# Graph attention with edge attributes on one core: gathers up to three groups ahead, one product for messages and attributes, and the merge of an item moved into the next step

## What is computed

```python
xl = (x @ Wl + bl).reshape(n, heads, outc)
e_feat = jax.nn.leaky_relu(xl[src] + (x @ Wr + br).reshape(n, heads, outc)[dst], NEG_SLOPE)
logits = jnp.einsum('ehc,hc->eh', e_feat, att)
m = jax.ops.segment_max(logits, dst, num_segments=n)
a = jnp.exp(logits - m[dst])
denom = jax.ops.segment_sum(a, dst, num_segments=n)
a = a / denom[dst]
out = jax.ops.segment_sum(xl[src] * a[:, :, None], dst, num_segments=n)
```

## Time and profile before

| | us |
|---|---|
| median of 3 runs | 8522.77 |
| lowest, highest | 8516.57, 8523.01 |
| profiled execution | 8491.84 |
| its span | 8489.9 |

### The profile page before, as it was taken

The page is one execution under the profiler, slowest core; times in us unless marked ns, Lnnn a source line. Parts: engine busy times, 40 slices in busy tenths (PEclk is TensorE's granted clock), DMA queues, the critical chain, the costliest instruction groups (busy, mean ns, idle before and its releaser), DMA issues.

```text
span 8489.9 us, 109176 instructions
## 1 busy us (share of the span) xinstructions
PE 4879.8 (57%) x24176; PEld 4286.7 (50%) x24176; DVE 5222.4 (62%) x16308; ACT 4307.0 (51%) x10681; POOL 4740.8 (56%) x4843
## 2 busy tenths in 40 slices
PE   4666666666666655555555555545555555544446
PEld 3565656565656544444444444444444444444444
DVE  5555565656565656766666667655555555555556
ACT  3444444444454545555555555545555555555546
POOL 3555555555555545666666666656666666666640
PEclk7666666666666666766767767666666666666666
DMA  5333333333333322322322323222222222222221
GB/s 147 94 100 91 96 97 97 97 96 97 96 98 95 98 67 74 79 76 76 77 75 77 82 77 78 76 66 72 77 71 71 72 72 72 76 73 72 72 61 50
DMA packets 460163, 697.83 MB, mean 82 GB/s; under 512 B 140781, under 2 KB 330019, under 8 KB 460101
## 3 DMA queue, kind: packets, MB, share of 16 engines
q0 software_dynamic: 154752, 327.15, 16.9%
q1 hardware_dynamic: 305349, 370.00, 14.2%
HBM read 638.95 MB, written 57.76 MB: 82 GB/s over the span
## 4 chain that ended last, share of the span: by engine, by line
PE 33%; issue 27%; DVE 22%; another core or an unknown queue 7%; ACT 6%; POOL 3%; DMA 2%; SPq 0%; DVEq 0%; ACTq 0%; POOLq 0%
PE PS L791 14%; PE PS L763 10%; PE PS L783 6%; DVE z L1186 3%; POOL xl_g L706 3%; DVE am L1193 3%; DVE msg L1285 2%; ACT distT L931 2%; ACT ST L936 2%; DVE relu_logit L1202 1%; ACT dist L906 1%; PE PS L749 1%; DMA xl_g<-xl_tab,edges 1%; DVE relu_logit L1205 1%
## 5 line engine op out<-in xcount | busy, mean ns | idle before, releaser
L706 POOL DMA_INDIRECT xl_g<-xl_tab,edges x4836 | 4740.0, 980 | 3485.8 <-DVE z L1186 1689.1
L763 PE MATMUL PS<-xr_w,ST 128*128 128x132 f32 x9672 | 2054.2, 373 | 2160.7 <-issue 1278.8
L763 PEld LDWEIGHTS PS<-xr_w,ST 128*128 128x128 f32 x9672 | 1778.9, 269 | 2455.4 <-issue 1735.2
L791 PE MATMUL PS<-msg,S 128*128 128x137 f32 x9672 | 1829.7, 352 | 936.8 <-issue 648.7
L791 PEld LDWEIGHTS PS<-msg,S 128*128 128x128 f32 x9672 | 1710.6, 257 | 1017.6 <-issue 1012.0
L1186 DVE TENSOR_TENSOR z<-PS,xl_g 128x528 f32<-128x528 f32 x1302 | 856.6, 658 | 1428.1 <-DMA xl_g<-xl_tab,edges 823.2
L906 ACT ACTIVATE dist<-node_row,neg_dst 128x128 f32<-128x128 f32 x4836 | 1534.5, 386 | 0.0
L931 ACT ACTIVATE distT<-dst_all,neg_node 128x512 f32<-128x512 int16 x1302 | 884.0, 679 | 1029.7 <-DVE neg_dst L1179 725.5
L909 ACT ACTIVATE S<-dist 128x512 f32<-128x512 f32 x1302 | 780.4, 599 | 839.9 <-remote 625.2
L1193 DVE SCALAR_TENSOR_TENSOR am<-z,att_relu 128x512 f32<-128x512 f32 x1302 | 860.8, 661 | 115.0 <-remote 94.1
L936 ACT ACTIVATE ST<-distT 128x512 f32<-128x512 f32 x1302 | 780.0, 599 | 42.6 <-ACT distT L931 1.4
(11 more groups left out here) (220 smaller groups left out, 3691.4 us busy)
## 6 DMA issues: line engine op xcount, KB each, us to landing
dst_all<-dst_short SPq DMA_DIRECT2D x186, 832.0 KB
xl_g<-xl_tab,edges POOLq DMA_INDIRECT x4836
ea<-edge_attr SPq DMA_DIRECT2D x124, 432.0 KB
ea<-edge_attr SPq DMA_DIRECT2D x62, 384.0 KB
xr_w<-xr_tab SPq DMA_DIRECT2D x186, 66.0 KB
dst_r<-dst_rows SPq DMA_DIRECT2D x186, 64.0 KB
node_row<-node_id SPq DMA_DIRECT2D x186, 64.0 KB
state<-t_new SPq DMA_DIRECT2D x126, 68.0 KB
```

Of the source, the lines that this page charges most:

```text
L706: pool.indirect_dma_start(xl_g[:, q, t, :], None, xl_tab[stage][:, :], bass.IndirectOffsetOnAxis(idx[:, q, t:t + 1], 0))\
L763: last = pe.matmul(zp[(q + g) % 3][:, n, :], ST[:, t, :], xr_w[:, q, :], start=True, stop=True)
L791: last = pe.matmul(agg_ps, S[:, q, t, :], msg[:, t, :], start=t == 0 and stage > 0, stop=t == TILES - 1)
```

## The change

1. `BEHIND` is 3: the gathers of a group wait for `z` three groups before, not two.
2. The attributes are loaded into the message tile itself: `msg` has 233 columns for each edge instead of 137, and in stage 0 one product (`sums`, 233 columns) takes the place of two (137 and 96) and of the product with zeros that opened the bank. There is one buffer for attributes, where there were two; they are loaded for item k + 1 as the sums of item k have read them, in parts of 12, 8 and 6 tiles, each element now 384 bytes long.
3. The merge (`new_max`, the exponential, `new_state`) and `turn_norm` are no longer at the end of the step that closes an item, but in groups 0 and 1 of the next step (`merges`); the logits of turned rows move from group 2 to group 5 on DVE, and PE's products for turned rows from groups 0 and 1 to 2 and 3. Each stage has one step more at its end.
4. ACT takes the groups of `ST` earlier relative to `S`.
5. SP loads the next item first, then stores the merged window, then loads attributes, then stores turned rows.

The space for `ST` and `dst_all` is shared with a later buffer, which changes no instruction in the stages.

```diff
-EA_CUTS = {3: range(0, 9), 4: range(9, 18), 5: range(18, TILES)}
+EA_GROUPS = (range(0, 3), range(3, 5), range(5, NG))
+EA_CUTS = [range(GROUPS[g[0]][0], GROUPS[g[-1]][-1] + 1) for g in EA_GROUPS]
-BEHIND = 2
+BEHIND = 3
...
-        msg = sb("msg", [P, TILES, MSG])
+        msg = sb("msg", [P, TILES, MSG + D_EDGE])
...
             with eng.Fori(1, last_pair) as i:
-                step(item(i, 1), item(i, 0), item(i + 1, 0), turned(i - 1, 1))
-                step(item(i + 1, 0), item(i, 1), item(i + 1, 1), turned(i, 0))
+                step(item(i, 1), item(i, 0), item(i + 1, 0), item(i - 1, 1))
+                step(item(i + 1, 0), item(i, 1), item(i + 1, 1), item(i, 0))
...
+                sp.dma_start(msg[:, a:b, MSG:MSG + D_EDGE],
+                             edge_attr[bass.ds(ch, 1), :, a * D_EDGE:b * D_EDGE].rearrange("a p (t f) -> (a p) t f", f=D_EDGE)).then_inc(ea_loaded, 16)
+
+            def next_attributes(k):
+                ch = chunk(k + 1)
+                sp.sem_inc(spacer, 1)
+                for m, tiles in enumerate(EA_CUTS):
+                    if m < len(EA_CUTS) - 1:
+                        sp.wait_ge(ea_read, k * (len(EA_CUTS) - 1) + (m + 1))
+                    else:
+                        sp.wait_ge(agg_done, k + 1)
+                    load_attributes(ch, tiles)
...
+                def store_merged(k, q):
+                    here, ahead = window(k - 1), window(k)
+                    sp.sem_inc(spacer, 1)
+                    sp.wait_ge(item_done, before + k)
+                    sp.dma_start(state[stage][bass.ds(here, P), :], st_new[:, 1 - q, 0:width]).then_inc(state_stored, 16)
+                    sp.wait_ge(state_stored, (before + k) * 16)
+                    sp.dma_start(st_old[:, q, 0:width], state[stage][bass.ds(ahead, P), :]).then_inc(state_loaded[q], 16)
...
+                def item_step(k, q, behind):
+                    logits_made(k)
                     load_item(k + 2, q, stage)
+                    if behind:
+                        store_merged(k, q)
+                    if first:
+                        next_attributes(k)
                     if turns and behind:
                         store_turned(k - 1, stage, before)
...
+                        if g == 0 and stage == 0:
+                            pe.wait_ge(ea_loaded, v * (16 * len(EA_CUTS)))
                         pe.wait_ge(onehot_done[g], v * 2)
                         pe.wait_ge(msg_done[g], v + 2)
+                        to, width = (sums_ps, MSG + D_EDGE) if stage == 0 else (agg_ps, MSG)
                         for t in GROUPS[g]:
-                            last = pe.matmul(agg_ps, S[:, q, t, :], msg[:, t, :], start=t == 0 and stage > 0, stop=t == TILES - 1)
+                            last = pe.matmul(to, S[:, q, t, :], msg[:, t, 0:width], start=t == 0, stop=t == TILES - 1)
...
-                        if turned and g < 2:
-                            (turn_rows, turn_products)[g]()
                         if closes and g == 2:
                             close("max")
+                        if turned and g in (2, 3):
+                            (turn_rows, turn_products)[g - 2]()
...
+                    if merges and g == 1:
+                        new_state()
+                    if closes and g == 1:
+                        carries()
                     if closes and g == 2:
                         shift()
-                    if turned and g == 2:
+                    if turned and g == 5:
                         turn_logits()
                     if opens:
                         relu_att(g)
+                    if merges and g == 0:
+                        new_max()
...
-                    if closes and g == NG - 1:
-                        new_max()
+                    if closes and g == 0:
+                        runs()
+                    if turned and g == 1:
+                        turn_norm()
```

More of the change, by code:

```diff
@@ L455, in item @@
                 return q, pairs * (2 * stage) + 2 * i + (q + 1), pairs * stage + i + 1
-            def turned(i, q):
-                return item(i, q) if stage < LAYERS - 1 else None
             step(None, None, item(0, 0), None)
@@ L598, in _, with logits_made @@
                     load_window(windows[q], q, stage)
-                    if first:
-                        ch = chunk(q)
-                        for tiles in EA_CUTS.values():
-                            load_attributes(ch, q, tiles)
+                if first:
+                    ch = chunk(0)
+                    for tiles in EA_CUTS:
+                        load_attributes(ch, tiles)
                 sp.dma_start(st_old[:, 0, 0:ROW if first else ROW_L], state[stage][bass.ds(windows[0], P), :]).then_inc(state_loaded[0], 16)
-                def item_step(k, q, behind):
-                    here, ahead = window(k), window(k + 1)
+                width = ROW if first else ROW_L
+                def store_merged(k, q):
[5 more added lines that the diff above has]
+                    sp.dma_start(st_old[:, q, 0:width], state[stage][bass.ds(ahead, P), :]).then_inc(state_loaded[q], 16)
+                def logits_made(k):
                     sp.wait_ge(onehot_done[NG - 1], (before + k + 1) * 2)
@@ L736, in _, with pe_step @@
             for stage in range(LAYERS):
-                def pe_step(opens, closes, begins, turned):
+                def pe_step(opens, closes, begins, merges):
+                    turned = merges if stage < LAYERS - 1 else None
                     def turn_rows():
@@ L879, in _, with act_step @@
             for stage in range(LAYERS):
-                def act_step(opens, closes, begins, turned):
+                def act_step(opens, closes, begins, merges):
+                    turned = merges if stage < LAYERS - 1 else None
                     def turn_hidden():
@@ L955, in act_step @@
                     if opens:
-                        for g in range(2, NG):
+                        onehotT(opens, 2)
+                    if merges:
+                        rescales()
+                    if opens:
+                        onehot(0)
+                        onehotT(opens, 3)
+                        onehot(1)
+                        onehotT(opens, 4)
+                    if turned:
+                        turn_hidden()
+                    if closes:
+                        alphas()
+                    if opens:
+                        onehotT(opens, 5)
+                        onehot(2)
+                    if turned:
+                        turn_copies()
+                    if opens:
+                        onehot(3)
+                        onehotT(opens, 6)
+                        for g in range(4, NG):
                             onehot(g)
-                            if g + 3 < NG:
-                                onehotT(opens, g + 3)
                     if opens:
@@ L1170, in node_logits, with edge_step @@
                 assert n.n == LOGIT_STEPS, n.n
-            def edge_step(stage, opens, closes, begins, turned):
+            def edge_step(stage, opens, closes, begins, merges):
+                turned = merges if stage < LAYERS - 1 else None
                 def prepare():
@@ L1306, in new_state @@
                 def new_state():
-                    q, v, use = closes
+                    q, v, use = merges
                     dve.wait_ge(rescale_done, v)
@@ L1363, in edge_step @@
                 for g in range(NG):
-                    if closes and g == 0:
-                        runs()
-                    if closes and g == 1:
-                        carries()
                     if opens:
@@ L1394, in edge_step @@
                     add_linear(NG - 1)
-                if closes:
-                    new_state()
-                    if stage < LAYERS - 1:
-                        turn_norm()
             for r in range(ROUNDS):
@@ L1417, in _ @@
             for stage in range(LAYERS):
-                pipeline(dve, stage, pairs, last_pair, lambda opens, closes, begins, turned: edge_step(stage, opens, closes, begins, turned))
+                pipeline(dve, stage, pairs, last_pair, lambda opens, closes, begins, merges: edge_step(stage, opens, closes, begins, merges))
             dve.wait_ge(hid_bias, 1)
```

102 lines of the change are left out of this document (34 added, 68 removed).

## The result

The changed kernel took 8656.05 us (8643.97 to 8664.46, 4 runs) beside 8522.89 us for the kernel before (8516.57 to 8528.51): a ratio of 1.0149 with an interval of 1.0136 to 1.0163. It is slower by 1.5%, where 6% less was forecast. Later runs of the same two kernels add the other half of the result: in other sessions on the chips, the kernel before takes 7200 us and the changed one 6716 us, a ratio of 0.9325 (0.9309 to 0.934). What decides is whether the slow stretches of the prediction occur in a session.

What follows compares the result with a forecast made beforehand. Waits in a ring of engines, not one engine, bound the kernel. Steps of 41.5, 40.5 and 39.3 us gave 7521, plus 61 and 372 for 7954 us of span, forecast 7985 us; 8-in-10 range 7400 to 8400 us.

Steps and rivals of the forecast that it cites:

- slow stretches: Spans near item turns where every engine but POOL gets instructions slowly; 4.8, 1.6, 7.9 us a step by stage before.
- The ring of the helpers: Time the engines beside POOL need per step without slow stretches: 35 us in stage 0, 34 in stage 1, 29 in stage 2.
- the rival in which stretches go away: DVE's group 1 pause suffices for POOL; steps of 35, 34 and 33.3 us, 6807 us in all; chance 0.13.
- The way from the last `z` to the next item's first: DVE node numbers, two ACT operations, PE expansion between items: taken at 4.5 us, bounds 3.5 and 7.9 us.
- The merge's wait: Idle time before the merge's first DVE operation, mostly for PE's last sums: 836 us, to become next to nothing.
- The single product: PE's 233-column product in stage 0, replacing two: 2 to 3 us less a step, at least 0.42 us each, hidden.
- The loads of attributes: Stage 0 loads in 384-byte pieces: costed at nothing because needed much later; 5 us a step without that cover.
- The price of the slow stretch: Time a stretch adds to each step: 6.5 us in stages 0 and 1, 10.3 us in stage 2.
- I take 0.7 of a group left: Gathers POOL may still issue when the stretch starts, stages 0 and 1: 3.5 + 3 = 6.5 us a step.
- a stretch in each step of stage 1: Sign: PE's single passes with 0.7 us before each, once a step in stage 1 too, 6 to 11 us long.
- The rival that the stretches grow: Up to 12 gathers instead of 8 after onset; 13 us stretches, steps 48, 47, 42 us, 8958 us; chance 0.10.
- That POOL must rest: Rival: stretches enforce POOL's idle time of 8.7 and 7.7 us; steps 42, 42, 41 us, 8215 us; chance 0.22.

Runs made afterwards that it cites:

- s3_rest: Changed kernel plus one GpSimd fill of 3.97 us a step before the gathers of group 1, in a session with stretches: 8529.00 us, ratio 0.9958 to the kernel before.
- m4_after: The changed kernel itself, unaltered, traced in a session without slow stretches: 6718.27 us, ratio 0.9328 to the kernel before.

## Why the prediction was wrong

**The ring of the helpers** was not put too low, and more than that no run shows. The steps of 35, 34 and 33.3 us of the rival in which stretches go away are 34.9, 34.0 and 33.5 us in the sessions without them, and its 6807 us stand beside 6716 measured. But in those sessions POOL, with its 0.3 us between two gathers, is idle for only 1.0, 0.1 and 0.1 us a step: in stages 1 and 2 the 33.3 us of gathers set the step, and the helpers' ring may be any length below it. That the 34 us of stage 1 came out as 34.0 (33.3 from item to item) is luck. In stage 0 the step from item to item is 34.1 us, beside the 35 of the sum. The way from the last `z` to the next item's first, taken at 4.5 us, is 6.7, 4.1 and 4.8 us there. The merge's wait fell from 836 to 25 us, as forecast.

**The single product** was taken right. In a session without stretches PE makes 44 passes of 233 columns in 9.27 us at 2.4 GHz (a granted clock of 0.95 in that stretch), 0.42 us for a tile's two, the lower bound that the prediction worked out. The loads of attributes, in pieces of 384 bytes, show no wait of their own in the rows, so no run here shows what short pieces cost; nor does SP's new order or the extra merging step.

```profile
1127.98 9.27 PE L796 MATMUL PS<-msg,S 128*128 128x233 f32 x44
```

**The price of the slow stretch** is the term that failed. Forecast were 6.5, 6.5 and 10.3 us; since the waits would give back a few of these, 121.3 - 102.3 = 19 us for three steps. Measured are 31.2: 12.4, 11.0 and 7.8 us by stage. The step of the argument at fault is the one from "It starts within one gather of the turn" to "I take 0.7 of a group left". The turn of two items was not what starts the stretch. In the kernel before POOL resumed at the gather of index 8 of an item, and the stretch began 17 or 18 gathers on, between 25 and 0. With the merge's long group 1 behind it POOL resumes later, at index 20, and the stretch begins 13 or 14 gathers on, at index 7 or 8 of the next item. From there POOL has four or five gathers left to its limit at index 12, 1.1 groups instead of 0.7, and the others are slow for these and for 3 us more: 8.7 and 9.8 us a step on PE in stages 0 and 1. That is 2.2 and 3.3 us more than the 6.5 us of the sum.

The second half of the miss is that the sum took the stretch on PE for the whole price. In stages 0 and 1 a step loses 12.4 and 11.0 us. Of these, 10.0 and 11.0 stand between the last `z` of an item and the next one's first (16.7 and 15.1 us, against 6.7 and 4.1 without stretches), where DVE and ACT are slow as well and the first `z` waits 912 us in all for PE's expansion, which comes behind the stretch. In stage 2, DVE stands twice a step. So three of the signs that the prediction named came out as it said (the merge's wait; a stretch in each step of stage 1, 6 to 11 us long; waits for gathered rows under 400 us) and the steps did not.

**The rival that the stretches grow** had the direction and the mechanism, POOL's gathers after the onset, with a mean of 10.3 us as the point from which the change loses. The mean loss measured is 31.2/3 = 10.4 us, and the sign turned. That the two agree so closely is partly luck: its rings were 32.7 us in the mean, measured are 102.4/3 = 34.1, and not two groups were left but 1.1. It had a chance of 0.10, which was too little: the evidence for it, one more group after the onset, was in the rows, and a row for "0.7 of a group" was not. **That POOL must rest** gave steps of 42, 42 and 41 us. In stage 2 all kernels come near to that (41.2 to 42.6 us); in stage 0 they take 43.0 to 47.8 us. POOL spends 8 to 15 us a step beyond the 33.3 us of gathers in every session with stretches, but that is not one fixed rest.

**What was not asked at all** is whether the stretches belong to the kernel. In the seven sessions here the same two programs have them or not by the session, all runs of a session alike. Not one of the prediction's rows could show it, as all came from one session.

**Open** is what makes the difference between the sessions, and by what way gathers slow the other engines' instructions. From POOL's resuming to the onset PE issued some 110 to 135 loads and passes in both kernels' first traces in stages 0 and 1 (counted from the records; the number depends on where the onset is put), but 150 and more in stage 2 of the changed one. So a fixed stock of instructions explains only part, and s3_rest shows that to relieve one engine does not relieve the step. One explanation can be narrowed down: that the engines wait for instructions to be fetched by DMA. The changed kernel's page counts

```profile
q8 instruction: 19, 0.31, 0.0%
q14 instruction: 42, 0.34, 0.0%
```

transfers of instructions in the whole execution, and m4_after, without a single stretch, has 19 and 43. They stand near the start of the program and of each stage and in the last part: from 330 to 2960 us of the changed kernel's first trace, where 56 of the 60 stretches of stage 0 lie, the trace records none. So the stretches are not slow transfers of this kind; whatever supplies instructions inside the loop is not seen in these traces.

## What to carry to other kernels

A gain that lets one engine work in longer streaks is worth what the others can do meanwhile: read from the trace what happens to them in the longest streak so far, and price the change by that, not by the waits it removes. Measure a kernel in several sessions before a few per cent are believed; here one edit is worth 6.7% less time or 1.5% more. Where one allowance moves a loss about, try its next values too: four groups ahead took 1.1% less time than the kernel before where there are stretches, where three took 1.5% more, and the two are equal where there are none.

## What the runs showed of the hardware

In three of seven sessions, the first among them, the engines beside GpSimd (PE, DVE, ACT and SP) start instructions only every 0.7 us or a multiple of it, for 2 to 15 us at a time, while GpSimd issues indirect gathers in a long streak: mostly from 11 to 18 gathers after it resumed, and until up to some 3 us after it stops (2.9 us in the step of stage 1 shown, 2.3 and 0.1 us in the two halts of stage 2). In the traces of the other four sessions the same streak of 26 gathers and more slows nothing. The busy times of the two kernels are alike in both kinds within 1% for DVE, ACT and POOL; PE's are 4% (changed) and 11% (before) longer where there are stretches. The transfers of instructions that the traces count are as many in both kinds, and none is recorded while most stretches run. The whole time is 18% longer for the kernel before and 29% for the changed one.
